# Softmax division moved behind the product with V, and the attention output transposed by DMA instead of being computed transposed

## The reference

```python
# x, ctx: (8, 128, 256); 16 query heads, 4 key/value heads, head size 128
q, k, v = LN(x) @ wq, LN(x) @ wk, LN(x) @ wv     # q, k: rms norm and rotary
k_ctx, v_ctx = ctx @ wk_ctx, ctx @ wv_ctx        # k_ctx: rms norm
scores = einsum('blhd,bmhd->bhlm', q, [k_ctx, k]) / sqrt(128) + causal
probs = softmax(scores)
out = einsum('bhlm,bmhd->blhd', probs, [v_ctx, v])
x = x + out.reshape(8, 128, 2048) @ wo
x = x + moe(LN(x))   # 8 experts of width 128, the 2 best of each token, and a shared one
```

## Time and profile before

| | |
|---|---|
| device time, 3 runs | median 381.09 us (379.98 to 385.2) |
| span of the profiled execution, first to last instruction | 381.2 us |
| mean granted TensorE clock | 0.984 of full speed |
| busy shares | PE 90%, DVE 87%, ACT 71%, POOL 50% |
| start of out_proj, rows 1 to 7 | 81.4, then every 35.8 to 36.0 us up to 297.0 |
| start of out_proj(7), in the tail | 323.9 us |
| DMA | 13.5 MB in all, most of it before 50 us |

### The profile page before, as it was taken

One profiled execution on the slowest core, in us unless ns is written; L12 is line 12 of the kernel. 1 busy time (PEld: TensorE's weight loads), 2 busy tenths in 40 slices (PEclk: granted clock), 3 DMA queues, 4 the chain that ended last, 5 costly groups with the idle time before them and its releaser, 6 DMA issues.

```text
span 381.2 us, 7816 instructions
## 1 busy us (share of the span) xinstructions
PE 343.1 (90%) x2471; PEld 235.3 (62%) x2476; DVE 331.7 (87%) x577; ACT 271.3 (71%) x913; POOL 191.6 (50%) x266
## 2 busy tenths in 40 slices
PE   6678697699999989999999999999999999988994
PEld 5354455376567666866685577558666768664572
DVE  1687999998999899899989998999899896759653
ACT  3667879576986797698759876986797566067562
POOL 3377666663766386528454554655284401234330
PEclk9998989999999999999999999999999998999998
DMA  5966000000030003000000000000000000000011
GB/s 174 379 208 220 17 0 0 3 2 14 3 110 0 14 0 110 15 0 0 0 14 0 0 0 14 0 0 0 0 0 1 2 0 2 2 0 3 13 45 56
DMA packets 11604, 13.50 MB, mean 35 GB/s; under 512 B 824, under 2 KB 9024, under 8 KB 11584
## 3 DMA queue, kind: packets, MB, share of 16 engines
q1 hardware_dynamic: 11584, 13.25, 10.7%
HBM read 12.20 MB, written 1.05 MB: 35 GB/s over the span
## 4 chain that ended last, share of the span: by engine, by line
DVE 40%; PE 34%; issue 12%; ACT 6%; POOL 3%; DMA 2%; SPq 1%; DVEq 1%; ACTq 0%; POOLq 0%
PE proj L1342 10%; DVE probs L970 9%; DVE nmax L957 6%; DVE pT_lo L895 4%; PE pt_ps L1318 3%; DVE q_t L886 3%; PE proj L1174 3%; PE o_ps L1328 3%; PE sc_ps L1284 3%; DVE q_t L888 3%; DVE qT_lo L895 2%; ACT probs L531 2%; PE turn L1263 2%; DMA wq<-in_L_xattn_wq_dram 2%; PE proj L1506 2%
## 5 line engine op out<-in xcount | busy, mean ns | idle before, releaser
L531 ACT ACTIVATE probs<-sc_ps,nbias,q_r 128x256 f32<-128x256 f32 x128 | 70.8, 574 | 3.4 <-DVE nbias L961 3.4
L758 POOL TENSOR_TENSOR q_rot<-q_t 128x512 f32<-128x512 f32 x32 | 42.8, 1336 | 36.2 <-DVE q_t L888 35.4
L970 DVE TENSOR_SCALAR probs<-probs,rden 128x256 f32<-128x256 f32 x80 | 57.1, 763 | 1.1
L442 ACT ACTIVATE pT_hi<-pt_ps 128x512 f16<-128x512 f32 x64 | 34.8, 597 | 14.5 <-PE pt_ps L1318 14.5
L1174 PE MATMUL proj<-wq_hi,xT 128*128 128x512 f16 x128 | 39.2, 389 | 3.4 <-DVE wq_lo L879 3.0
L895 DVE SCALAR_TENSOR_TENSOR pT_lo<-pt_ps,pT_hi 128x512 f16<-128x512 f32 x64 | 40.9, 680 | 1.2 <-ACT pT_hi L442 1.2
L475 ACT ACTIVATE q_junk<-proj 128x128 bf16<-128x128 f32 x128 | 34.0, 296 | 9.5 <-DVE q_t L888 9.5
L957 DVE TENSOR_REDUCE nmax<-sc_ps 128x4 f32<-128x1024 f32 x32 | 38.8, 1212 | 1.5 <-PE sc_ps L1306 1.5
L1318 PE MATMUL pt_ps<-ident,probs 128*128 128x128 f32 x256 | 34.9, 281 | 2.2 <-DVE probs L970 2.0
L708 POOL TENSOR_TENSOR q_r<-q_me,power 128x4 f32<-128x4 f32 x32 | 34.2, 1069 | 2.5
L1342 PE MATMUL proj<-wo_hi,oT_hi 128*128 128x256 f16 x128 | 34.9, 273 | 0.0
(11 more groups left out here) (217 smaller groups left out, 940.6 us busy)
## 6 DMA issues: line engine op xcount, KB each, us to landing
wq<-in_L_xattn_wq_dram SPq DMA_DIRECT2D x4, 512.0 KB, 8.8
w<-in_L_ffn_w_dram SPq DMA_DIRECT2D x2, 1024.0 KB, 10.2
wq<-in_L_xattn_wo_dram SPq DMA_DIRECT2D x1, 2048.0 KB, 8.4
ctx_b<-in_ctx_dram SPq DMA_DIRECT2D x8, 128.0 KB, 2.0
out_dram<-x_all SPq DMA_DIRECT2D x4, 256.0 KB, 2.2
x_all<-in_x_dram SPq DMA_DIRECT2D x1, 896.0 KB, 12.6
wkc<-in_L_xattn_wk_ctx_dram SPq DMA_DIRECT2D x1, 512.0 KB, 4.1
wk<-in_L_xattn_wk_dram SPq DMA_DIRECT2D x1, 512.0 KB, 5.0
```

The lines of the kernel that those rows point to most:

```text
L442: return nc.scalar.activation(out_, in_, ACT.Copy, scale=scale)
L531: last = nc.scalar.activation(probs[:, h, :], sc_ps[:, h, :], ACT.Exp, bias=nbias[:, h:h + 1], scale=q_r[:, g, h:h + 1], accum_out=den[:, ...
L758: nc.gpsimd.tensor_tensor(q_rot[:], q_t1[:], q_t2[:], ALU.add).then_inc(q_added, 1)
L970: last = nc.vector.tensor_scalar(probs[:, h, :], probs[:, h, :], rden[:, h:h + 1], None, ALU.mult)
```

## The change

Probabilities stay undivided. `turn_probs` waits for the exponentials alone. `mix` takes the transposed probabilities of one head as the stationary operand and V as the moving one, 128 columns at a time: 24 matmuls instead of 6, and `o_ps` has tokens on partitions. There VectorE divides it by the sums while it reads PSUM (`o_scale`, into fp32 `o_n`), ScalarE writes the high half from `o_n` (`o_copy`), GpSimd the low half (`o_rest`), and SyncE transposes each half by DMA into `oT_hi` and `oT_lo` (`o_turn`, 128x512 fp16 each, 64 DMAs in all). `out_proj(b)` waits at its start for all transposes of its row. The sums, their reciprocals and the new tiles have two buffers each, by g % 2. GpSimd loses its part of `normalise` and gets `o_rest` of the previous group at the end of each slot. The router's `ahead` and `tied` share the memory of `probs`. The loads of `ctx` and of the expert weights are issued between the transposes.

```diff
@@ tiles
-        den = sb("den", [P, R])
-        rden = sb("rden", [P, R])
+        den = sb("den", [P, 2, R])
+        rden = sb("rden", [P, 2, R])
+        o_n = sb("o_n", [P, 2, GW])
+        o_hi = sb("o_hi", [P, 2, GW], FP16)
+        o_lo = sb("o_lo", [P, 2, GW], FP16)
...
+        duels = probs[:].rearrange("p h k -> p (h k)").rearrange("p (a t e f) -> p a t e f", a=2, e=E, f=E)
+        ahead, tied = duels[:, 0], duels[:, 1]
@@ SyncE
-            next_ctx(2)
-            next_ctx(3)
...
+            def o_turn(b, g):
+                if g == 0 and b:
+                    sp.wait_ge(wo_done, b)
+                for src, dst, made, turned in ((o_hi, oT_hi, o_high, d_oT_hi), (o_lo, oT_lo, o_low, d_oT_lo)):
+                    sp.wait_ge(made, G * b + g + 1)
+                    sp.dma_start_transpose(dst[:, g, :].rearrange("p (h t) -> p h t", h=R),
+                                           src[:, g % 2, :]).then_inc(turned[g % 2], 16)
+
+            for b in range(B):
+                for g in range(G):
+                    o_turn(b, g)
+                    if g == 0 and b + 2 < B:
+                        next_ctx(b + 2)
...
@@ ScalarE
             def o_copy(u, g):
-                act.wait_ge(pv_done, u + 1)
-                copy(oT_hi[:, g, :], o_ps[:], O_SCALE / (P_SCALE * V_SCALE)).then_inc(o_high, 1)
+                act.wait_ge(o_scaled, u + 1)
+                seen(act, d_oT_hi[g % 2], o_slot_free(u, g))
+                copy(o_hi[:, g % 2, :], o_n[:, g % 2, :]).then_inc(o_high, 1)
@@ GpSimd
-            def normalise(b, g):
...
+            def o_rest(u, g):
+                pool.wait_ge(o_high, u + 1)
+                seen(pool, d_oT_lo[g % 2], o_slot_free(u, g))
+                nc.gpsimd.tensor_tensor(o_lo[:, g % 2, :], o_n[:, g % 2, :], o_hi[:, g % 2, :],
+                                        ALU.subtract).then_inc(o_low, 1)
@@ VectorE
-            def o_low(u, g):
-                dve.wait_ge(o_high, u + 1)
-                low(oT_lo[:, g, :], o_ps[:], O_SCALE / (P_SCALE * V_SCALE), oT_hi[:, g, :]).then_inc(o_ready, 1)
+            def o_scale(u, g):
+                dve.wait_ge(pv_done, u + 1)
+                dve.wait_ge(s_rden, u + 1)
+                seen(dve, o_low, u - 1)
+                nc.vector.scalar_tensor_tensor(out=o_n[:, g % 2, :].rearrange("p (h d) -> p h d", h=R),
+                                               in0=o_ps[:].rearrange("p (h d) -> p h d", h=R),
+                                               scalar=O_SCALE / (P_SCALE * V_SCALE),
+                                               in1=rden[:, g % 2, :].unsqueeze(2).broadcast_to([P, R, P]),
+                                               op0=ALU.mult, op1=ALU.mult).then_inc(o_scaled, 1)
...
-            def normalise(b, g):
+            def inv_den(b, g):
+                dve.wait_ge(s_exp, G * b + g + 1)
+                nc.vector.reciprocal(rden[:, g % 2, :], den[:, g % 2, :]).then_inc(s_rden, 1)
@@ TensorE
-                pe.wait_ge(s_probs, u + 1)
-                pe.wait_ge(s_probs2, count_pool(b, g - 1))
+                pe.wait_ge(s_exp, u + 1)
...
-                    for i, (v, p) in enumerate(((v_hi, pT_hi), (v_lo, pT_hi), (v_hi, pT_lo))):
-                        last = nc.tensor.matmul(o_ps[:], v[:, a, g * P:(g + 1) * P], p[:, a, :],
-                                                start=(a == 0 and i == 0), stop=(a == 1 and i == 2))
+                    for h in range(R):
+                        head = slice(h * P, (h + 1) * P)
+                        for i, (p, v) in enumerate(((pT_hi, v_hi), (pT_hi, v_lo), (pT_lo, v_hi))):
+                            last = nc.tensor.matmul(o_ps[:, head], p[:, a, head], v[:, a, cols],
+                                                    start=(a == 0 and h == 0 and i == 0),
+                                                    stop=(a == 1 and h == R - 1 and i == 2), skip_group_check=True)
...
             def out_proj(b):
-                pe.wait_ge(o_ready, G * b + G - 1)
...
+                for turned in d_oT_hi + d_oT_lo:
+                    pe.wait_ge(turned, 16 * (2 * b + 2))
                 for h in range(H):
-                    if h == H - R:
-                        pe.wait_ge(o_ready, G * b + G)
```

More of the change, by code:

```diff
@@ L296, in xattn_moe_kernel @@
         s_rden = sem("s_rden")
[L297 to L304, removed]
         p_turned = sem("p_turned")
@@ L308, in xattn_moe_kernel @@
         pv_done = sem("pv_done")
+        o_scaled = sem("o_scaled")
         o_high = sem("o_high")
-        o_ready = sem("o_ready")
+        o_low = sem("o_low")
+        d_oT_hi = [sem(f"d_oT_hi{i}") for i in range(2)]
+        d_oT_lo = [sem(f"d_oT_lo{i}") for i in range(2)]
         wo_done = sem("wo_done")
@@ L371, in xattn_moe_kernel, with o_slot_free @@
         half_e = (slice(0, E // 2), slice(E // 2, E))
+        def o_slot_free(u, g):
+            return 16 * ((u - g) // G * 2 + g // 2) if isinstance(u, int) else ((u - g) * 8 + 16 * (g // 2))
         block = stack.enter_context(nc.Block())
@@ L417, in next_ctx @@
                 sp.dma_start(ctx_b[:], ctx[b, :, :]).then_inc(d_ctx, 16)
-            next_ctx(2)
-            next_ctx(3)
[L423 to L430, removed]
+            def o_turn(b, g):
[10 more added lines that the diff above has]
+                        next_ctx(b + 2)
+                    if (b, g) == (1, 2):
+                        sp.wait_ge(w1_cast, 4)
+                        sp.dma_start(w1_32[:], w3.rearrange("e h d -> h e d")).then_inc(d_w3, 16)
+                    if (b, g) == (2, 2):
+                        sp.wait_ge(w3_cast, 4)
+                        sp.dma_start(w1_32[:].rearrange("p e (c h) -> p (e c) h", c=DC),
+                                     w2.rearrange("e (c p) h -> p (e c) h", p=P)).then_inc(d_w2, 16)
             with sp.Fori(0, B // 2) as i:
@@ L526, in exps @@
                 seen(act, p_turned, u)
+                seen(act, s_rden, u - 1)
                 for h in range(R):
@@ L815, in row @@
                                                 ALU.subtract).then_inc(wo_low2, 1)
+                    if g or not first:
+                        o_rest(G * b + g - 1, (g - 1) % G)
                     if cast:
@@ L849, in e_scale @@
                                         ALU.mult).then_inc(e_scaled2, 1)
+            o_rest(G * B - 1, G - 1)
             e_scale(0)
@@ L1075, in row @@
                     if g or not first:
-                        o_low(u - 1, (g - 1) % G)
+                        o_scale(u - 1, (g - 1) % G)
                     if g == 2 and not last:
@@ L1137, in _ @@
             xn_copy(2)
-            o_low(G * B - 1, G - 1)
+            o_scale(G * B - 1, G - 1)
             dve.wait_ge(c_low, 1)
```

16 lines of the change are left out of this document (4 added, 12 removed).

## The result

The changed kernel takes 405.14 us (median of 4 runs, 401.69 to 406.98), beside 380.89 us for the kernel before on the same chip (4 runs, 379.98 to 385.2). The ratio is 1.061, with a 95% interval of 1.053 to 1.069: slower. The profiled execution is one of the quicker ones: its span is 401.6 us, against 381.2 in the profile before, and the time recorded for it is 403.36 us. A recorded time is some 1.8 us longer than the span of the same execution. So the traces account for 20.4 us of the 24.3 between the medians.

The account below looks back on a forecast made before the run. It took row 0 as bound by VectorE, and later rows by VectorE and TensorE together. Row 0 -1.0, six row periods +18.6, last row and tail +5.4 gave +23.0 on 381.2: 404.2 us, range 389 to 428 us.

Parts of the forecast that it names:

- Stretch A: From v to out_proj, rows from 1 on: out_proj waits for group 3's chain and landing, a loss of 2.6 us a row.
- Stretch B: Slots 2 and 3: o_copy and o_rest delay TensorE's turns, less gaps that close before turn_probs and elsewhere; net +0.5 us a row.
- TensorE's gaps: Idle gaps in TensorE's timeline of one later row, added up to 2.4 us, the most that relief of VectorE could take off.
- rival 1: Faster: the landing hides behind other work and TensorE's gaps close instead, 20 us at most, half of it 371 us; chance 0.05.
- VectorE "falls to some 27.5 us a row": In a later row, without the division's products, VectorE's busy time falls to some 27.5 us and bounds nothing there.
- Row 0: First row: 3 us gained from VectorE's relief, less 2.0 us for the wait before out_proj in row 1; net -1.0 us.
- Last row and tail: out_proj(7) starts 4.1 us later, a clock fall behind its wait costs 1.7 us, a closed gap returns 0.4: +5.4 us.
- mix at 0.055 us a matmul: mix's 24 matmuls of 128 columns start 0.055 us apart, 1.32 us in all, no change from 1.29 us.
- rival 2: No change: landing of about 1.2 us and the costs in slots 2 and 3 hidden, 385 us; chance 0.12.
- rival 3: mix runs at half pace, 0.11 us a matmul, 430 us; chance 0.11.
- rival 4: The clock falls in every row behind the wait before out_proj, 1.7 us each in six rows, 414 us; chance 0.17.
- rival 5: Transposes land only after 6 us or more, as serial halves, 428 us; chance 0.10.

Follow-up runs that it names:

- e1_grace: The changed kernel with out_proj waiting at its start only for groups 0 to 2, and for group 3 ahead of its last 12 matmuls: 392.35 us.
- e5_slot0: The changed kernel with slot 0 reordered: o_scale before v_low, o_copy before v_copy, o_rest right behind q_add: 391.1 us.
- e2_relief: The kernel before with the division by the sums left out on VectorE and GpSimd, reciprocal kept, nothing added: 370.96 us.
- e6_slot23: The changed kernel with kc_scale and k_squares before o_copy in slot 2, and group 1's o_rest behind q_add of slot 3: 400.49 us.
- in the second: Second profile, from running the changed kernel once more, unedited: 405.04 us.
- e8_mix: The kernel before with only mix changed to 24 matmuls of 128 columns, probabilities stationary, division kept: 382.44 us.
- e9_all: The changed kernel with the edits of e1_grace, e5_slot0 and e6_slot23 together: 376.39 us, ratio 0.986 to the kernel before.
- e7_dose: The changed kernel with each low half's transpose issued only after its high half has landed: 423.3 us.
- e3_plain: The changed kernel with plain DMA copies of the same 128 KB in place of the transposes: 399.71 us.

## Why the prediction was right

- **The verdict and the size** (+23.0 us, 404.2 us): 405.14 us measured. The prediction was right in its verdict and near in its size, but that the median comes within 1 us is partly luck. It added its sum to a span (381.2 us), and the result is a time, some 1.8 us longer than the span of the same execution. Its 404.2 is 2.6 us above the span of the first profile, and that execution is 1.8 us quicker than the median. Of the parts, row 0 was too low and the rows too high; both differences are below.
- **Stretch A, +2.6 us a row:** the mechanism was right, the size near. The chain was 3.95 us against 4.0; the landing, taken as 3.0, was 2.4. With 2.4 the step gives +2.0, and the timeline shows +2.2. e1_grace and e5_slot0 each took most or all of the wait of the rows away, by two different ways. The clause on vc_low was right too: q is delayed by 0.97 us and still ends ahead of the landing.
- **Stretch B, +0.5 us a row:** it came out as +0.2 (period +2.4 less A's 2.2), but from two larger numbers. The relief of turn_probs is worth 0.9 us a row (e2_relief: 35.0 against 35.9), not 0.5, and the new work in slots 2 and 3 costs about 1.1, of which e6_slot23 gets back 0.6.
- **TensorE's gaps, "2.4 us" a row:** the idle times of TensorE in that row add up to 1.5 us, which is also 36.00 less the 34.48 busy. No part of the forecast uses the 2.4, only rival 1's bound of 20 us, which was too wide.
- **VectorE "falls to some 27.5 us a row":** wrong for the change (29.89), right for the division alone (27.72 in e2_relief). The prediction took only the durations of the new instructions, and left out that VectorE's instructions with two SBUF inputs last longer beside GpSimd's. In a later row nbias takes 0.99 us beside `o_rest` (0.16 alone), and k_sum 1.70 beside `q_add` (1.23 before the change). Nothing in a later row hung on it, since TensorE bounds there.
- **Row 0, -1.0 us:** 0.0 in the first profile, whose clock fell once there, and +1.8 in the second, with two falls as before the change. This is the step that failed, by 2.8 us where the clock is equal. Stretch A took 2.1 us, predicted as 2.0 (0.98 and 1.15 us of idle time before out_proj(0)). The relief, counted as 3 us, did not show. TensorE's busy time is as before the change (44.8 us against 44.6), and its idle time grew from 11.0 to 13.1 us. That is stretch A's 2.1 us, less the 0.79 us gap that is gone, and 0.8 us more behind the small product beside GpSimd's split (3.26 us for 2.44). Nothing is left over for a relief.
- **Last row and tail, +5.4 us:** 3.3 + 2.1 = 5.4 in the first profile, 4.9 + 1.7 = 6.6 in the second, where the last row has a fall of the clock as the kernel before has. That the first sum is met exactly is luck. In the first profile the wait was 4.58 us, predicted as 5, the clock stood at half for 6.8 us from 341.1 on, not 3.4, and out_proj(7) took 7.99 us (342.21 to 350.20) instead of about 5.3. In the second the clock stood at half for 3.4 us and the cost was 1.7, as predicted.
- **mix at 0.055 us a matmul:** 0.056. e8_mix puts 24 for 6 at 0.2% of the time. o_rest took 1.17 us, predicted as 1.3.
- **The rivals.** 1 and 2 fell with a landing of 2.4 us; yet rival 1's other condition, that TensorE has other work in that place, was sound: e9_all gives it that work, and 29 us come back. 3 fell with e8_mix. 4 did not happen, though e7_dose shows that it would have with 1.2 us more of wait. 5 fell with the measured landing.

By parts, then: the new waits and orders cost 34 us, the division's removal gives back 10; of the 34, 13 go with out_proj's early wait for group 3 alone (e1_grace), 14 with the order of slot 0 alone (e5_slot0), 5 with that of slots 2 and 3 alone (e6_slot23), and 29 with all three (e9_all), which leave every instruction in place. Of the 5 us that are left between e9_all and e2_relief the later rows hold most, 1 us each; no run takes the new chain apart there.

## What to carry to other kernels

Here a DMA that carries a value from one engine to another cost its landing only where the consumer had nothing else to do. Before judging such a change, look for the first instruction that needs the last piece, and put the wait there and the producers first in their lists. Three changes of order turned 6% slower into 1.4% faster here, with the same instructions, though one of them also mended a wait that the kernel before had. Before comparing two profiles stretch by stretch, count the falls of the clock in each: here one was worth 1.6 to 1.8 us. Work handed to GpSimd is not free for VectorE: see which instructions with two SBUF inputs run beside it.

## What the runs showed of the hardware

- A transposing DMA of 128x512 fp16 from SBUF to SBUF landed 2.4 us after its issue (median of 64, 4.5 us at most), a plain copy of the same 128 KB after 2.0. Its issue took 1.19 to 1.35 us on the SP queue, that of the plain copy 0.46 in most (e3_plain).
- Waits of 0.97 and 1.16 us with 1.5 us of matmuls between them left TensorE at 2.4 GHz in five of the six later rows, and so did 0.97 and 1.68 in the sixth. With the second wait at 2.37 us TensorE stood at 1.2 GHz for 3.4 us behind it in each row. Around and behind 4.58 us of idle time it stood there for 6.8 us in one execution of the changed kernel (the first 26 of out_proj(7)'s 48 matmuls started 0.213 us apart instead of 0.109) and for 3.4 us in another.
- A stretch of 3.4 us at 1.2 GHz in row 0 made the same code 1.6 to 1.8 us longer, with equal idle time of TensorE.
- A VectorE product of 4 columns lasted 3.44 us while GpSimd ran one long subtraction, and 0.16 without it.
